# A Perceiver-style block on one core: another order of the tensor work in cross-attention, with the first context-value product behind the second transposes

## The reference, cut to what matters

```python
def _L0_xattn_ref(queries, keys, values, Wq, bq, Wk, bk, Wv, bv, Wo, bo):
    q = (queries @ Wq.T + bq).reshape(B, L, H, E)
    k = (keys @ Wk.T + bk).reshape(B, S, H, E)
    v = (values @ Wv.T + bv).reshape(B, S, H, E)
    scores = jnp.einsum('blhe,bshe->bhls', q, k)
    attn = jax.nn.softmax(scores * scale, axis=-1)
    out = jnp.einsum('bhls,bshe->blhe', attn, v).reshape(B, L, H * E)
    return out @ Wo.T + bo
x = x + _L0_xattn_ref(_layernorm(x, axis=-1), ctx_1024, ctx_1024, ...)
x = x + _L0_attn_ref(_layernorm(x, axis=-1), ...)
x = x + _L0_ffn_ref(_layernorm(x, axis=-1), ...)
```

## Time and profile before

| what | value |
|---|---|
| median of the runs | 896.88 us |
| the profiled execution | 896.43 us, span 894.6 us |
| granted TensorE clock, mean over the span | 0.996 |
| busy: TensorE matmuls, weight loads | 861.2 us (96%), 724.1 us |
| busy: VectorE, ScalarE, GpSimd | 745.5 us, 707.0 us, 483.2 us |
| transposes of probabilities L349, 1024 | 126.6 us busy |
| row maxima L470, 256 | 158.8 us busy, 683 ns each |
| exponentials L513, 512 | 237.3 us busy, 487 ns each |

### The profile page before, as it was taken

How to read it: one execution, slowest core, us unless ns; L and a number is a source line. 1 busy time by engine, 2 the same in 40 slices (tenths; PEclk the granted TensorE clock), 3 DMA queues, 4 the chain that set the end, 5 groups by cost and what they waited for, 6 DMA issues and landing times.

```text
span 894.6 us, 28711 instructions
## 1 busy us (share of the span) xinstructions
PE 861.2 (96%) x9750; PEld 724.1 (81%) x9750; DVE 745.5 (83%) x1551; ACT 707.0 (79%) x2077; POOL 483.2 (54%) x710
## 2 busy tenths in 40 slices
PE   7999999999999999999999988999999998999997
PEld 6888888888888889888888977888888885666664
DVE  6878878878878878878878776899999988999995
ACT  4788887777787777778777775888888877999996
POOL 3333334355454554433443226787878864777775
PEclk9999999999999999999999998999999999999999
DMA  6222111111111011111111100000000000000011
GB/s 193 91 90 84 42 47 30 43 49 35 36 47 41 30 47 41 47 29 41 47 41 30 36 1 2 2 3 0 0 1 0 1 1 2 29 32 30 30 36 35
DMA packets 31635, 31.84 MB, mean 36 GB/s; under 512 B 3280, under 2 KB 30800, under 8 KB 31568
## 3 DMA queue, kind: packets, MB, share of 16 engines
q1 hardware_dynamic: 30448, 30.47, 11.1%
q10 hardware_dynamic: 1120, 0.59, 0.2%
HBM read 26.86 MB, written 4.19 MB: 35 GB/s over the span
## 4 chain that ended last, share of the span: by engine, by line
PE 76%; ACT 11%; issue 5%; DVE 5%; POOL 2%; DMA 0%; DVEq 0%; ACTq 0%; POOLq 0%; SPq 0%
PE psum L349 12%; PE psum L319 9%; PE psum L304 9%; PE psum L336 8%; PE psum L375 6%; PE psum L681 5%; ACT probs L1056 3%; PE psum L719 3%; PE psum L730 3%; PE psum L387 3%; ACT probs L513 3%; PE psum L291 3%; PE psum L773 2%; PE psum L700 2%; PE psum L357 2%
## 5 line engine op out<-in xcount | busy, mean ns | idle before, releaser
L513 ACT ACTIVATE probs<-psum,nmax 128x256 f32<-128x256 f32 x512 | 237.3, 487 | 89.9 <-DVE nmax L470 89.9
L470 DVE TENSOR_REDUCE nmax<-psum 128x2 f32<-128x512 f32 x256 | 158.8, 683 | 7.5 <-PE psum L336 7.3
L544 POOL TENSOR_TENSOR rm<-rinv,hm_sb 128x256 f32<-128x256 f32 x64 | 39.7, 621 | 214.8 <-DVE rinv L447 214.8
L349 PE MATMUL psum<-id_sb,probs 128*128 128x128 f32 x1024 | 126.6, 275 | 0.5
L537 POOL TENSOR_TENSOR cl<-c_sb,ch 128x512 fp32r<-128x512 f32 x64 | 81.6, 1275 | 77.6 <-ACT ch L488 77.6
L349 PEld LDWEIGHTS psum<-id_sb,probs 128*128 128x128 f32 x1024 | 114.4, 141 | 4.0 <-ACT probs L513 4.0
L494 ACT ACTIVATE probsT<-psum 128x512 f32<-128x512 f32 x160 | 89.4, 614 | 33.8 <-PE psum L349 32.5
L513 ACT ACTIVATION_READ_ACCUMULATOR probs<-psum,nmax 128x1 f32 x512 | 112.3, 219 | 0.0
L336 PE MATMUL psum<-k_sb,qb 32*128 32x256 f32 x1024 | 81.3, 401 | 4.2 <-DVE qb L431 1.2
L440 DVE COPY probsT<-psum 128x512 f32<-128x512 f32 x96 | 65.5, 682 | 11.2 <-PE psum L349 9.3
L336 PEld LDWEIGHTS psum<-k_sb,qb 32*128 32x128 f32 x1024 | 53.9, 184 | 21.5 <-issue 15.6
(11 more groups left out here) (155 smaller groups left out, 2389.4 us busy)
## 6 DMA issues: line engine op xcount, KB each, us to landing
c_sb<-in_ctx_t SPq DMA_DIRECT2D x64, 256.0 KB, 2.8
x_sb<-in_x SPq DMA_DIRECT2D x32, 128.0 KB, 2.5
out<-y_sb SPq DMA_DIRECT2D x32, 128.0 KB, 1.7
w_all<-in_w_gate SPq DMA_DIRECT2D x1, 1024.0 KB, 5.1
w_all<-in_w_up SPq DMA_DIRECT2D x1, 1024.0 KB, 6.7
w_all<-in_w_down SPq DMA_DIRECT2D x1, 1024.0 KB, 5.9
wqkv_sb<-in_w_qkv SPq DMA_DIRECT2D x1, 768.0 KB, 5.2
wk_sb<-in_wk ACTq DMA_DIRECT2D x1, 256.0 KB, 4.0
```

The source lines that it names most:

```text
L349: last = nc.tensor.transpose(sp[g][:, c:c + P], probs[:, 2 * g + u, kh * P:(kh + 1) * P], id_sb[:])
L470: nc.vector.tensor_reduce(nmax[:, 2 * g:2 * g + 2], sp[g].rearrange("p (u s) -> p u s", u=2), AX.X, ALU.max, negate=True).then_inc(max_don ...
L513: nc.scalar.activation(probs[:, j, :], sp[g][:, u * S:(u + 1) * S], ACT.Exp, bias=nmax[:, j:j + 1], accum_out=rsum[:, j:j + 1]).then_inc(e ...
```

## The change

TensorE's body is reordered: R of (t,0) comes right behind the scores of (t,1), the values of (t+1,0) are computed whole ahead of the transposes of (t,1), and PV of (t,0) comes behind these transposes, directly ahead of the scores of (t+1,0). For this probsT gets one buffer for each sample (the second shares memory with hq), and the values of s = 0 one for even and one for odd tiles (the even ones in qT2[1]). XT always goes to the query bank mp instead of op. The contexts are split half a tile earlier: (t+1,1) in the first half of tile t and (t+2,0) in its second. Of the four copies of each transposed sample VectorE takes groups 0 and 2 and ScalarE 1 and 3, in both samples; before, sample 1 had one on VectorE and three on ScalarE. VectorE's order follows. SyncE starts the three feed-forward weight loads (SET3) in bodies 1 to 3 ahead of those of SET2. The diff, cut to its core:

```diff
-        v_sb = [sb(f"v_sb{s}", [P, 2, D]) for s in range(2)]
-        probsT = sb("probsT", [P, PAIRS, 2, P])
+        hq_all = sb("hq_all", [P, 2, INNER])
+        probsT = [sb("probsT", [P, PAIRS, 2, P])[:],
+                  hq_all[:].rearrange("p s n -> p (s n)").rearrange("p (g k q) -> p g k q", g=PAIRS, k=2)]
+        v_all = [sb("v_s1", [P, 2, D]), sb("v_s0", [P, 2, D]), qT2[1]]
+        v_slot = lambda s, odd: v_all[0] if s else v_all[1 if odd else 2]
-        xt_ps = op[:, D:2 * D].rearrange("p (k t) -> p k t", k=KT)
+        xt_ps = mp[:, 0:D].rearrange("p (k t) -> p k t", k=KT)
-        def pe_xt(pe, t, to):
+        def pe_xt(pe, t, to, n=None):
             pe.wait_ge(xn_done, t + 1)
-            if not isinstance(t, int) or t > 2:
-                pe.wait_ge(op_done, (t - 2) * 2)
+            if n is not None:
+                pe.wait_ge(qb_done, n * 4 + 4)
...
         def pe_r(pe, t, s):
             pe.wait_ge(rm_done, b + 1)
+            if s == 0 and (not isinstance(t, int) or t > 0):
+                pe.wait_ge(y_ev, t)
...
-        def pe_pv(pe, t, s, ahead2=True):
+        def pe_pv(pe, t, s, odd):
             b = t * 2 + s
-            if s == 0 and ahead2:
-                pe.wait_ge(x1h_done, t + 3)
-            if s == 0 and (not isinstance(t, int) or t > 0):
-                pe.wait_ge(y_ev, t)
+            if s == 0:
+                pe.wait_ge(r_ev, b + 1)
             pe.wait_ge(v_ev, b + 1)
             pe.wait_ge(o_ev, b)
-            pe.wait_ge(pt_dve, t * 3 + (2, 3)[s])
-            pe.wait_ge(pt_act, t * 5 + (2, 5)[s])
+            pe.wait_ge(pt_dve, t * 4 + s * 2 + 2)
+            pe.wait_ge(pt_act, t * 4 + s * 2 + 2)
...
-                pe.wait_ge(x1h_done, turned)
...
             b = t * 2 + s
-            for g in ((1, 3), (1, 2, 3))[s]:
+            for g in (1, 3):
...
-                if g == (2 if s == 0 else 3) and before is not None:
+                if g == 2 and before is not None:
                     act_r(a, *before)
...
                 body(0, 0)
-                for dst, src in SET2:
-                    sp_.dma_start(dst, src).then_inc(w2_in, 16)
                 for i, (dst, src) in enumerate(SET3):
                     body(1 + i, (1 + i) % 2)
                     sp_.dma_start(dst, src).then_inc(w3_in[i], 16)
+                for dst, src in SET2:
+                    sp_.dma_start(dst, src).then_inc(w2_in, 16)
...
                     pe_transpose(pe, t, 0)
                     if not first:
-                        pe_out(pe, t - 1, t + 3 if ahead2 else None)
+                        pe_out(pe, t - 1)
                     pe_scores(pe, t, 1, n, j)
-                    pe_pv(pe, t, 0, ahead2)
+                    pe_r(pe, t, 0)
                     if j == 1:
                         pe_q(pe, n + 1)
-                    pe_r(pe, t, 0)
                     pe_k(pe, t + 1, 0)
-                    pe_v(pe, t + 1, 0, (0,))
+                    pe_v(pe, t + 1, 0)
+                    if wsum:
+                        pe_wsum(pe, t)
                     pe_transpose(pe, t, 1)
                     if wsum:
-                        pe_wsum(pe, t)
-                    pe_v(pe, t + 1, 0, (1,))
+                        pe.wait_ge(wscale, 1)
+                    pe_pv(pe, t, 0, j)
                     pe_scores(pe, t + 1, 0, n + j, 1 - j)
-                    if wsum:
-                        pe.wait_ge(wscale, 1)
-                    pe_pv(pe, t, 1)
+                    pe_pv(pe, t, 1, j)
                     pe_r(pe, t, 1)
...
                     dve_k(v, t, 1)
+                    dve_v(v, t, 1, j)
                     dve_inverse(v, t, 0)
                     dve_pt(v, t, 0, (0, 2))
                     if not first:
                         dve_y(v, t - 1)
-                    dve_v(v, t, 1)
                     dve_max(v, t, 1)
                     if j == 1:
                         dve_q(v, n + 1)
-                    dve_o(v, t, 0)
-                    dve_inverse(v, t, 1)
-                    dve_pt(v, t, 1, (0,))
+                    dve_k(v, t + 1, 0)
+                    dve_v(v, t + 1, 0, 1 - j)
                     if scale:
                         dve_wscale(v)
-                    dve_k(v, t + 1, 0)
+                    dve_pt(v, t, 1, (0, 2))
+                    dve_inverse(v, t, 1)
+                    dve_o(v, t, 0)
                     if ahead3:
                         dve_stats(v, LN1, t + 3, x_sb[1 - j][:], (x_in[1 - j], (n + 2 + j) * 16))
-                    dve_v(v, t + 1, 0)
                     dve_max(v, t + 1, 0)
...
                     act_pt(a, t, 0)
-                    act_c(a, t + 1, 0)
+                    act_c(a, t + 1, 0 if first else 1)
...
-                    act_exp(a, t, 1, (t, 0))
+                    act_r(a, t, 0)
+                    act_exp(a, t, 1)
                     act_pt(a, t, 1)
-                    act_c(a, t + 1, 1)
+                    if first:
+                        act_c(a, t + 1, 1)
+                    if ahead2:
+                        act_c(a, t + 2, 0)
...
                     if ahead2:
+                        pool_xl1(p, t + 2, j)
                         pool_xb(p, t + 2, n + 1, j)
-                    if j == 0:
-                        pool_c(p, t + 1, 0)
-                    if ahead2:
-                        pool_xl1(p, t + 2, j)
-                    if j == 1:
-                        pool_c(p, t + 1, 0)
+                    pool_c(p, t + 1, 0 if first else 1)
...
                     pool_rm(p, t, 1)
-                    pool_c(p, t + 1, 1)
+                    if first:
+                        pool_c(p, t + 1, 1)
+                    if ahead2:
+                        pool_c(p, t + 2, 0)
```

More of the change, by code:

```diff
@@ L146, in block_kernel @@
         rinv2 = sb("rinv2", [P, 16])
-        p2T = probsT[:, 0:4, :, :].rearrange("p a b c -> p (a b) c")
+        p2T = probsT[0][:, 0:4, :, :].rearrange("p a b c -> p (a b) c")
         oT2 = sb("oT2", [P, KT, P])
@@ L177, in block_kernel @@
         fd = [sb(f"fd{s}", [P, 1]) for s in range(2)]
-        hq = [sb(f"hq{s}", [P, INNER]) for s in range(2)]
+        hq = [hq_all[:, s, :] for s in range(2)]
         hqT = sb("hqT", [P, IT, P], BF16)
@@ L306, in pe_k, with pe_v @@
             last.then_inc(k_mm, 1)
-        def pe_v(pe, t, s, halves=(0, 1)):
+        def pe_v(pe, t, s):
             b = t * 2 + s
[L311 to L315, removed]
+            pe.wait_ge(ch_done, b + 1)
+            pe.wait_ge(cl_done, b + 1)
+            pe.wait_ge(v_ev, b)
+            for kh in range(2):
                 keys = slice(kh * P, (kh + 1) * P)
@@ L320, in pe_v @@
                                                 start=n + k == 0, stop=n == 2 and k == KT - 1)
-            if 1 in halves:
-                last.then_inc(v_mm, 1)
+            last.then_inc(v_mm, 1)
         def pe_scores(pe, t, s, n, j):
@@ L375, in pe_pv, with pe_out @@
                         last = nc.tensor.matmul(op[32 * c:32 * c + 32, m * P:(m + 1) * P],
-                                                v_sb[s][:, kh, 32 * j:32 * j + 32],
-                                                probsT[:, 2 * c + m, kh, :], start=kh == 0,
+                                                v_slot(s, odd)[:, kh, 32 * j:32 * j + 32],
+                                                probsT[s][:, 2 * c + m, kh, :], start=kh == 0,
                                                 stop=kh == 1)
             last.then_inc(pv_mm, 1)
-        def pe_out(pe, t, turned=None):
+        def pe_out(pe, t):
             pe.wait_ge(o_ev, t * 2 + 2)
-            if turned is not None:
-                pe.wait_ge(x1h_done, turned)
             for k in range(KT):
@@ L414, in dve_xn, with dve_v @@
                                     ALU.subtract, ALU.mult).then_inc(ln.xn_done, 1)
-        def dve_v(v, t, s):
+        def dve_v(v, t, s, odd):
             v.wait_ge(v_mm, t * 2 + s + 1)
-            nc.vector.tensor_tensor(v_sb[s][:], v_ps, bv_sb[:].unsqueeze(1).to_broadcast([P, 2, D]),
+            nc.vector.tensor_tensor(v_slot(s, odd)[:], v_ps, bv_sb[:].unsqueeze(1).to_broadcast([P, 2, D]),
                                     ALU.add).then_inc(v_ev, 1)
@@ L439, in dve_pt @@
                 v.wait_ge(t_mm, b * 4 + g + 1)
-                nc.vector.tensor_copy(probsT[:, 2 * g:2 * g + 2, :, :].rearrange("p a b c -> p (a b c)"),
+                nc.vector.tensor_copy(probsT[s][:, 2 * g:2 * g + 2, :, :].rearrange("p a b c -> p (a b c)"),
                                       sp[g]).then_inc(pt_dve, 1)
@@ L491, in act_pt @@
             b = t * 2 + s
-            for g in ((1, 3), (1, 2, 3))[s]:
+            for g in (1, 3):
                 a.wait_ge(t_mm, b * 4 + g + 1)
-                nc.scalar.activation(probsT[:, 2 * g:2 * g + 2, :, :].rearrange("p a b c -> p (a b c)"),
+                nc.scalar.activation(probsT[s][:, 2 * g:2 * g + 2, :, :].rearrange("p a b c -> p (a b c)"),
```

(25 more changed lines are left out.)

18 lines of the change are left out of this document (8 added, 10 removed).

## The result

The changed kernel takes 931.3 us (median of 4 runs, 929.66 to 931.93) against 896.94 us for the kernel before beside it: a ratio of 1.038, 95% interval 1.036 to 1.040. The forecast was 907.6 us in a range of 895 to 912: the direction was right, the size was not, and the measured time lies far outside the range.

The account below looks back on a forecast made before the run. Tensor engine bound, busy 861.2 of 894.6 us. Second halves add 13.1, first halves return 1.9, 0.5 comes off: +10.7; with 896.43 and 0.45 that gives 907.6 us, range 895 to 912.

Parts of the forecast that it names:

- The direction and its mechanism: Behind PV0, o(t,0) and statistics delay the next scores' first maximum from 1.18 to 1.68 us after their start; slower, 0.68.
- o_prod and oT take 0.66 (395.54 to 396.20): On VectorE between PV0 and the next maxima: both instructions keep their old duration of 0.66 us at the new place.
- The margin of 0.11 us before PV1: At PV1, which now waits for o(t,0): o ends 0.97 us after the scores of (t+1,0) start, PV1 due at 1.08.
- Rival 3: Before PV1: o(t,0) could be 0.2 us late, the first maximum at 1.9, 0.2 more in 29 halves; 913 us, chance 0.08.
- XT's slack: XT, the transpose of the tile after next, waits 0.82 us for xn, which could swallow a pushed PV1.
- T1, S0' and the first halves: From scores of (t,1) to those of (t+1,0): 7.40 us even, 8.47 odd; the even tile's transposes wait 0.38.
- Contexts half a tile ahead … worth nothing: Before K of (t+1,0): context low part ends at 385.51, K starts at 386.05, so no tensor wait to remove; 0 us.
- Turned x in the query bank: At XT: dropping the waits on op_done and x1h_done gains nothing, since XT waits for xn.
- The copy moved to VectorE: One 0.69 us probsT copy a tile, ahead of o(t,0), which waits for PV0 anyway: covered; uncovered, 0.7 a tile.
- The range: Total time: 895 to 912 us at 8 in 10; the likeliest case alone 903 to 912.
- The chain of 4.23: From the first maximum over exponentials, r_sb, o_prod, oT and xn to XT: 4.23 us, unchanged by the change.

Follow-up runs that it names:

- e3: The changed kernel with VectorE's statistics of tile t+3 ahead of o(t,0) instead of behind it; 909.95 us, ratio 1.014 to the kernel before.
- e4: The changed kernel with GpSimd's low part of context (t+2,0) behind o(t,0) and the statistics ahead of it; 893.58 us, ratio 0.9965 to the kernel before.
- e1: The changed kernel with one more wait: GpSimd's subtraction for context (t+2,0) starts only after o(t,0) is done; 908.68 us, ratio 1.013 to the kernel before.
- e2: The changed kernel with each GpSimd context subtraction split into two 128x256 instructions instead of one 128x512; 916.59 us, ratio 1.022 to the kernel before.
- e7: The changed kernel with the contexts split when the kernel before did it, on ScalarE and GpSimd; 935.91 us, ratio 1.043 to the kernel before.
- e5: Against e4: XT of t+2 amid the transposes of (t,0), ScalarE's copies of it between its probsT copies; 884.43 us, ratio 0.9865 to the kernel before.
- e6: Against e4: the third probsT copy of sample 1 back on ScalarE; 893.67 us, ratio 0.996 to the kernel before.

## Why the prediction was right or wrong

*The direction and its mechanism: right.* The forecast put the loss on o(t,0) and the statistics between PV0 and the maxima of S0'. e3 and e4 show it: taking the statistics out of that place gives 21.4 us alone, and 15.1 us once oT is not held (908.68 to 893.58). The chain's measured length in e1 (first maximum at S0' + 1.71, forecast 1.68) and e1's time (908.7, forecast 907.6) confirm the sum. In e1 the lag from the tensor engine to o_prod was 0.07 rather than 0.15, o_prod and oT took 0.73 (351.98 to 352.71) rather than 0.66, and the statistics 0.84 (to 353.55) rather than 0.80. That the pair comes out so close (33.71 against 33.65) is partly luck: its first halves are 0.11 us shorter than forecast together, its second halves 0.16 longer (8.85 in even and 9.09 in odd tiles, where 8.89 was forecast for both).

*The step that failed: "o_prod and oT take 0.66 (395.54 to 396.20)".* With the subtraction of GpSimd beside it the same pair took 1.49 (366.23 to 367.72). The duration was taken from a row in which GpSimd stood idle, and the step was moved to a place where it does not: the text says what waits for o(t,0) and what it waits for, but never what runs on GpSimd at that moment. In the kernel before, ch of (t+1,1) is written behind the probsT copies, and GpSimd's subtraction follows, while o(t,0) was finished (389.70) some two microseconds earlier; both facts could be read off its timeline:

```profile
391.82 1.27 POOL L537 TENSOR_TENSOR cl<-c_sb,ch 128x512 fp32r<-128x512 f32 x1 [1.12 <-ACT ch L488]
```

Against the 0.73 us that the pair takes in e1, the hold costs 0.76 in a second half. Over 29 second halves that is 22 us, and e1 measured 22.6 of the 23.7 us between the forecast of 907.6 and the measured 931.3.

The Trainium skill has the rule ("SBUF — State Buffer", Who interferes with whom): a VectorE instruction with two SBUF inputs contends with a GpSimd instruction that reads SBUF, whichever issues first keeps the shared ports for the whole instruction and the other is blocked fully. The trace agrees with it for every subtraction: oT has two SBUF inputs and is held (1.10), the maxima read PSUM alone and keep their length (682 ns on average, before 683), and in e2 the hold ends with the half that was under way. o_prod, with one input in PSUM, keeps its 0.42, but it was issued ahead of the subtraction. The other order stands in the kernel before: the eviction of values at 391.87, one input in PSUM and one in SBUF, starts 0.05 behind the subtraction above and takes its usual 0.68. One place does not fit: in the last tile of the changed kernel oT starts at 572.43, while a small GpSimd instruction with two SBUF inputs (rstd, 128x1, 572.09 to 572.64 by its row) is under way, and takes 0.29. The prediction did not apply the rule to the operation that the change moves.

*The margin of 0.11 us before PV1: right as a place, wrong in size.* Rival 3 named a late o(t,0), which pushes PV1 and the maxima, and let XT's slack swallow the first. It had o 0.2 late and the kernel at 913; o was some 0.8 late. PV1 came 0.69 late, K1 and V1 with it, and XT still idled for 1.00 us in the odd tile and 0.74 in the even one. e3 shows that PV1's wait alone cost next to nothing, as said.

*T1, S0' and the first halves: right.* 7.32 and 8.45 on average against 7.40 and 8.47; T1 idle 0.30. PV directly ahead of scores takes 1.01 to 1.02 (365.08 to 366.10), the value that was taken from its other neighbour.

*"Contexts half a tile ahead … worth nothing": wrong.* It compared the end of cl, 385.51, with K0' at its old place, 386.05. In the new order K0' is due 1.25 after S1, at 385.04. e7's trace prices the earlier contexts at 0.25 us a pair, some 4 us: without them the changed kernel would be slower still.

*Turned x in the query bank, "nothing": right for the changed kernel,* but e5 depends on it. There XT stands among the transposes, with only two of their groups between it and the output projection, which writes the part of op that XT used before. No run has e5's order with the old bank, so what the new one is worth there is not shown.

*The copy moved to VectorE: right* (e6).

*The range.* It was built from the scatter of lags inside one mechanism. The error came from outside: no term of the sum was allowed to change its own duration.

*The chain of 4.23: right in even tiles, short in odd ones.* From the first maximum to XT it takes 4.17 in even and 4.41 in odd tiles of the changed kernel, so the odd second half is some 0.25 us longer (9.85 against 9.60 on average; in e4 8.56 against 8.32). Most of it stands between r_sb and o_prod of (t,1), in the even tile

```profile
388.24 0.39 ACT L503 ACTIVATE r_sb<-psum 128x256 f32<-128x256 f32 x1
388.72 0.42 DVE L456 TENSOR_TENSOR o_prod<-psum,r_sb 128x256 f32<-128x256 f32 x1 [0.54 <-issue]
```

and in the odd one

```profile
371.08 0.40 ACT L503 ACTIVATE r_sb<-psum 128x256 f32<-128x256 f32 x1
```

with o_prod at 371.77, shown above: 0.09 and 0.29 us behind r_sb's end. VectorE's bodies stand in loops of two (v.Fori), and o(t,1) of an odd tile is the first step of the next pass. Where no new pass begins behind an odd tile (tiles 7, 27 and 29) the gap is 0.09 as well. In the kernel before and in e6, whose VectorE bodies hold one copy less, it is 0.19 in the passes where the changed kernel has 0.29 (behind tiles 11 to 25; behind 3 and 5 all three have 0.19). So the gap goes with the step from one pass to the next; what it consists of, and why it grew, stays open.

## What to carry to other kernels

When a step moves, its duration moves with it only if its neighbours on the other engines do too: before pricing a VectorE instruction with two SBUF inputs at its old row, read what GpSimd runs at the new place, and for how long. An instruction pair that others wait for (here o_prod and oT, for PV1 and the maxima) should stand where the long GpSimd instructions do not, or these should wait for it; one semaphore wait on an engine with time to spare was worth 22.6 us here. And when work between two steps is taken out, check each input of the step behind against its new due time, not its old one.

## What the runs showed of the hardware that was not expected

- VectorE's 128x128 tensor_tensor with both inputs in SBUF took 1.10 us instead of 0.29 while GpSimd's 128x512 tensor_tensor on SBUF was under way, and ended 0.14 us behind it; with that instruction split in two it took 0.57 and ended 0.15 us behind the first half.
- VectorE instructions with one input in PSUM and one in SBUF were not lengthened: o_prod took 0.42 us with GpSimd's subtraction starting inside it, and 45 evictions of values in the kernel before that started inside such a subtraction took 0.68 to 0.69.
- VectorE's first instruction behind the back edge of its loop started 0.19 or 0.29 us after the instruction it waited for had ended, where the same instruction elsewhere started after 0.09.
